# A four-level attention and FFN block: the first batch's loads, copies and early splits rearranged

## The reference

```python
for lvl in range(LEVELS):
    outs.append(_mha(query[:, ::2 ** lvl, :], in_proj_w[lvl], in_proj_b[lvl], out_w[lvl], out_b[lvl]))
current = outs[-1]
for lvl in range(LEVELS - 2, -1, -1):
    current = _upsample_linear(current, outs[lvl].shape[1])
    current = current @ up_w[lvl].T + up_b[lvl] + outs[lvl]
x = _layernorm(x + current)
h = silu(x @ w1.T * s1) * (x @ w2.T * s2)
h = gelu(h @ h1.T * g1); h = gelu(h @ h2.T * g2)
x = _layernorm(x + h @ w3.T * s3)
```

## Time and profile before

| | us |
|---|---|
| median of 3 runs | 4289.43 |
| lowest and highest | 4281.64, 4312.08 |
| the profiled execution, its own time | 4283.97 |
| its span | 4282.2 |
| attention's part of the span, roughly | 0 to 2790 |

### The profile page before, as it was taken

One profiled execution on the slowest core, in us unless ns is written; L12 is line 12 of the kernel. 1 busy time (PEld: TensorE's weight loads), 2 busy tenths in 40 slices (PEclk: granted clock), 3 DMA queues, 4 the chain that ended last, 5 costly groups with the idle time before them and its releaser, 6 DMA issues. The chain is left out here.

```text
span 4282.2 us, 69980 instructions
## 1 busy us (share of the span) xinstructions
PE 3849.3 (90%) x20881; PEld 2139.0 (50%) x20881; DVE 2564.1 (60%) x4681; ACT 2484.3 (58%) x3261; POOL 1212.0 (28%) x1144
## 2 busy tenths in 40 slices
PE   4499989989989999999999999809999999999998
PEld 2234434333433433433333433207887777877887
DVE  2377777787787787787787788553333333333333
ACT  1367767767767767767767767724444434444443
POOL 4234444434534534534434442210000000000000
PEclk8799999999999999999999999959999999999999
DMA  5434343334344344344344343160000000000000
GB/s 176 116 71 103 98 89 88 104 79 103 102 79 104 105 85 93 113 88 85 118 86 91 111 91 57 34 232 12 12 20 11 11 11 21 11 11 11 14 17 11
DMA packets 308844, 307.48 MB, mean 72 GB/s; under 512 B 75168, under 2 KB 285280, under 8 KB 308192
## 3 DMA queue, kind: packets, MB, share of 16 engines
q1 hardware_dynamic: 299200, 293.59, 27.9%
q10 hardware_dynamic: 9216, 8.39, 0.6%
HBM read 202.28 MB, written 96.47 MB: 70 GB/s over the span
## 5 line engine op out<-in xcount | busy, mean ns | idle before, releaser
L760 ACT ACTIVATE a_probs<-a_p_s 128x1024 f32<-128x1024 f32 x1360 | 1324.9, 1020 | 592.0 <-PE a_p_s L1002 584.9
L841 DVE TENSOR_REDUCE a_part_max<-a_p_m 128x1 f32<-128x512 f32 x2048 | 1335.8, 680 | 421.5 <-PE a_p_m L1017 417.2
L1017 PE MATMUL a_p_m<-a_k_st,a_q_st 96*128 96x512 bf16 (+2 forms) x2944 | 1007.3, 375 | 177.8 <-DVE a_part_max L841 73.8
L1397 PE MATMUL p_h<-f_h_hi,f_w_hi 128*128 128x512 f32 x2048 | 811.5, 396 | 40.3 <-issue 38.3
L1002 PE MATMUL a_p_s<-a_q_st,a_k_st 98*128 98x512 bf16 (+2 forms) x2944 | 822.9, 367 | 17.4 <-DMA a_q_st<-a_neg_bf 11.6
L1397 PE MATMUL p_h<-f_h_lo,f_w_hi 128*128 128x512 f32 x2048 | 807.7, 394 | 1.6 <-issue 1.6
L1017 PEld LDWEIGHTS a_p_m<-a_k_st,a_q_st 96*128 96x128 bf16 x2944 | 257.8, 97 | 1072.5 <-DVE a_part_max L841 676.6
L1034 PE MATMUL a_p_o<-a_probs,a_v_aug 128*17 128x512 f32 (+2 forms) x5888 | 727.5, 573 | 0.8 <-ACT a_probs L760 0.8
L1366 DVE TENSOR_TENSOR f_h_lo<-f_h_f,f_h_hi 128x512 fp32r<-128x512 f32 x256 | 177.3, 692 | 723.4 <-ACT f_h_hi L1279 723.4
L841 DVE TENSOR_REDUCE a_row_max<-a_p_m 128x1 f32<-128x512 f32 (+2 forms) x672 | 439.9, 680 | 183.6 <-PE a_p_m L1017 177.7
L1277 ACT ACTIVATE f_h_f<-p_h,f_sc 128x512 f32<-128x512 f32 x256 | 176.6, 690 | 584.4 <-PE p_h L1397 584.3
(11 more groups left out here) (116 smaller groups left out, 4604.5 us busy)
## 6 DMA issues: line engine op xcount, KB each, us to landing
qk_scratch<-a_qk_bf SPq DMA_DIRECT2D x96, 384.0 KB, 2.6
a_w_lo<-wqkv_inner SPq DMA_DIRECT2D x32, 768.0 KB, 4.4
a_q_st<-qk_scratch SPq DMA_DIRECT2D x192, 128.0 KB, 6.2
a_k_st<-qk_scratch SPq DMA_DIRECT2D x192, 128.0 KB, 6.5
a_q_st<-qk_scratch SPq DMA_DIRECT2D x336, 64.0 KB, 2.7
a_k_st<-qk_scratch SPq DMA_DIRECT2D x336, 64.0 KB, 2.7
a_a_lo<-a_attn SPq DMA_DIRECT2D x384, 32.0 KB, 2.0
a_o_lo<-wo_inner SPq DMA_DIRECT2D x24, 512.0 KB, 4.2
```

The source lines that it names most:

```text
L760: act.activation(probs[:, s % 2, 2 * p:2 * p + 2, :], p_s[:, 2 * p:2 * p + 2, :], ACT.Exp, scale=HD ** -0.5).then_inc(exp_done.sem, 1)
L841: dve.reduce_max(out, src, AX.X).then_inc(max_read.sem, 1)
L1017: ins = pe.matmul(p_m[:, n % 2, r * size:(r + 1) * size], q_st[0:ROWS, unit.place, j, q * 128:(q + 1) * 128], k_st[0:ROWS, unit.halves[kb] ...
L1397: ins = pe.matmul(out, a, c, start=first and n == 0, stop=last and n == len(terms) - 1)
```

## The change

The opening of batch 0 is arranged anew.

- x of batch 0 and the weights of level 2 go from the inputs straight into idle room: `x_first` and `w_first` are views of `probs`, free until step 0. The weights of level 1 go early into `w_second`, a view of `attn`; the later load task only waits for it and counts. Rounding and cut read from there in batch 0 (`w_raw`).
- x is loaded, rounded and cut in halves of tokens (0 to 511, 512 to 1023) in place of halves of features, in every batch. In batch 0 the second half is loaded behind the weight copies, and rounded and cut six steps after the first, which puts it between projections 0 and 1 in ScalarE's list. TensorE waits for the second half only at level 0.
- The three constant loads move behind the first weights. `row` has a semaphore of its own. VectorE fills one place of `k_st`'s ones (2x2048), and a DMA repeats it to the seven others; GpSimd's fill goes.
- The four weight copies are issued together before x's second half. wo and the seven copies of x become tasks `xcopy`, at steps 1, 4.2, 7.4 and so on to 23.4.
- Level 3's weights are loaded at -10.9 and projected at -5.7, level 0's at -5.2 and -1.35, with 1.2 steps between its projections. Stack 7 stands at 4.5. In SyncE's list the marker for level 1's weights comes ahead of the store of projection 0.
- Projections 0 to 5 of batch 0 have their second and third pieces made on VectorE. VectorE's shift of `v` is 0.4 in place of 0.3.

```diff
--- before.py
+++ after.py
@@ -210,10 +210,11 @@
+EARLY = 6
...
-    "dve": {"v": .3, "row": .3, "out": .3},
+    "dve": {"proj": .35, "v": .4, "row": .3, "out": .3},
@@ -234,9 +235,9 @@
-    load_at = {2: -36, 1: -22, 3: -11.5, 0: 2.5} if first else {2: CUT_POINT - STEPS + .05}
-    proj_at = {2: -28, 1: -16, 3: 1, 0: 6} if first else {}
-    gap = {2: 1, 1: 1, 3: .5, 0: .5} if first else {2: 1.5, 1: 2, 3: 1.5, 0: 2}
+    load_at = {2: -36, 1: -25.9, 3: -10.9, 0: -5.2} if first else {2: CUT_POINT - STEPS + .05}
+    proj_at = {2: -28, 1: -16, 3: -5.7, 0: -1.35} if first else {}
+    gap = {2: 1, 1: 1, 3: .5, 0: 1.2} if first else {2: 1.5, 1: 2, 3: 1.5, 0: 2}
@@ -262,13 +263,15 @@
-    p.append((load_at[2] - .01, "x", 0))
-    p += [(load_at[2] + 3 + .5 * c, "xcut", c) for c in range(2)]
+    p += [(load_at[2] - .01, "x", 0), (load_at[2] + .02 if first else load_at[2] - .005, "x", 1)]
+    if first:
+        p += [(1 + 3.2 * n, "xcopy", n) for n in range(B)]
+    p += [(load_at[2] + 3 + (6 if first else .5) * n, "xcut", n) for n in range(2)]
...
-        stack_at = {0: at[0] + 2.4, 1: at[1] + 2.4, 2: at[3] + 2.4, 3: at[3] + 2.5, 4: at[5] + 2.4, 5: at[5] + 2.5, 6: at[6] + 2.4, 7: at[10] + 2.25}
+        stack_at = {0: at[0] + 2.4, 1: at[1] + 2.4, 2: at[3] + 2.4, 3: at[3] + 2.5, 4: at[5] + 2.4, 5: at[5] + 2.5, 6: at[6] + 2.4, 7: 4.5}
@@ -317,7 +320,7 @@
-    before = [(STEPS + at, kind, 1, n) for at, kind, n in opening if (kind, n) in early]
+    before = [(STEPS + at, kind, 1, n) for at, kind, n in opening if (kind, n) in early or kind == "xcopy"]
@@ -376,6 +379,8 @@
+        x_first, w_first = probs[:, 0, :, :].rearrange("p (c u) t -> p c (u t)", c=2), probs[:, 1, :, :].rearrange("p h t -> p (h t)")[:, 0:QKVCOLS]
+        w_second = attn[:, :, :].rearrange("p r t -> p (r t)")
@@ -391,11 +396,11 @@
-        w_copied, o_copied = [sig(f"w_copied{n}", 0, 16) for n in range(4)], sig("o_copied", 0, 16)
-        x0_copied, x_copied = sig("x0_copied", 0, 16), sig("x_copied", 0, 16)
+        w_copied, o_copied, x_copied = [sig(f"w_copied{n}", 0, 16) for n in range(4)], sig("o_copied", 0, 16), sig("x_copied", 0, 16)
+        w_early, ones_in = sig("w_early", 0, 16), sig("ones_in", 0, 16)
...
-        const_in, const_done, set_done = sig("const_in", 0, 16), sig("const_done", 0), sig("set_done", 0)
-        x_loaded, x_hi_done, x_lo_done = sig("x_loaded", 1, 16), sig("x_hi_done", 2), sig("x_lo_done", 2)
+        const_in, row_in, const_done, set_done = sig("const_in", 0, 16), sig("row_in", 0, 16), sig("const_done", 0), sig("set_done", 0)
+        x_loaded, x_hi_done, x_lo_done = [sig(f"x_loaded{n}", 1, 16) for n in range(2)], sig("x_hi_done", 2), sig("x_lo_done", 2)
@@ -432,6 +437,10 @@
+        def w_raw(it, n):
+
+            return (w_first, w_second)[n] if it == 0 and n < 2 else w_lo[:, :].bitcast(F32)
+
@@ -459,12 +468,6 @@
-                sp.dma_start(col[:, :, :], cols).then_inc(const_in.sem, 16)
-                sp.dma_start(row[:, :, :], rows).then_inc(const_in.sem, 16)
-                sp.dma_start(ident[:, :], ident_in).then_inc(const_in.sem, 16)
-
-                sp.dma_start(wqkv[W_ORDER[0], :, :], wqkv_in[W_ORDER[0], :, :]).then_inc(w_copied[0].sem, 16)
-                sp.dma_start(xt[0, :, :], xt_in[0, :, :]).then_inc(x0_copied.sem, 16)
@@ -473,36 +476,50 @@
-
...
+                            half = slice(n * W, (n + 1) * W)
...
-                                sp.wait_ge(x0_copied.sem, 16)
+                                sp.dma_start(x_first[:, :, half], xt_in[0, :, half].rearrange("(c p) t -> p c t", p=128)).then_inc(x_loaded[n].sem, 16)
...
-                            hold()
-                            sp.dma_start(x_lo[:, :, :].bitcast(F32), xt[number(it), :, :].rearrange("(c p) t -> p c t", p=128))\
-                              .then_inc(x_loaded.sem, 16)
+                                hold()
+                                sp.dma_start(x_lo[:, :, half].bitcast(F32), xt[number(it), :, half].rearrange("(c p) t -> p c t", p=128))\
+                                  .then_inc(x_loaded[n].sem, 16)
+                        elif kind == "xcopy":
+                            if n == 0:
+                                sp.dma_start(wo[:, :, :], wo_in[:, :, :]).then_inc(o_copied.sem, 16)
+                            else:
+                                sp.dma_start(xt[n, :, :], xt_in[n, :, :]).then_inc(x_copied.sem, 16)
...
-
...
-                            if it == 0:
+                            if it == 0 and n > 1:
...
-                            sp.dma_start(w_lo[:, :].bitcast(F32), wqkv[lvl, :, :]).then_inc(w_loaded.sem, 16)
-                            if it == 0 and n < 2:
-                                for i in (1,) if n == 0 else (2, 3):
+                            if it == 0 and n == 0:
+                                sp.dma_start(w_first, wqkv_in[lvl, :, :]).then_inc(w_loaded.sem, 16)
+                            elif it == 0 and n == 1:
+                                sp.wait_ge(w_early.sem, 16)
+                                sp.sem_inc(w_loaded.sem, 16)
+                            else:
+                                sp.dma_start(w_lo[:, :].bitcast(F32), wqkv[lvl, :, :]).then_inc(w_loaded.sem, 16)
+                            if it == 0 and n == 0:
+                                sp.dma_start(col[:, :, :], cols).then_inc(const_in.sem, 16)
+                                sp.dma_start(ident[:, :], ident_in).then_inc(const_in.sem, 16)
+                                sp.dma_start(row[:, :, :], rows).then_inc(row_in.sem, 16)
+                                sp.dma_start(w_second, wqkv_in[W_ORDER[1], :, :]).then_inc(w_early.sem, 16)
+                                sp.wait_ge(zeroed.sem, 2)
+                                hold()
+                                sp.dma_start(k_st[ROWS:ROWS + 2, 1:HALVES, :, :].rearrange("p b h t -> p b (h t)"),
+                                             k_st[ROWS:ROWS + 2, 0, :, :].rearrange("p h t -> p (h t)").unsqueeze(1).broadcast_to((2, HALVES - 1, HG * W))).then_inc(ones_in.sem, 16)
+                                for i in (1, 2, 3, 0):
...
-                            elif it == 0 and n == 2:
-                                sp.dma_start(wo[:, :, :], wo_in[:, :, :]).then_inc(o_copied.sem, 16)
-                                for b in range(1, B):
-                                    sp.dma_start(xt[b, :, :], xt_in[b, :, :]).then_inc(x_copied.sem, 16)
@@ -614,10 +631,8 @@
-                pool.memset(k_st[ROWS:ROWS + 2, :, :, :], 1.0).then_inc(set_done.sem, 1)
+                pool.memset(minus_half[:, :], -0.5).then_inc(set_done.sem, 1)
...
-                pool.memset(minus_half[:, :], -0.5).then_inc(set_done.sem, 1)
-                pool.wait_ge(set_done.sem, 3)
@@ -625,18 +640,19 @@
-                            pool.tensor_tensor(out=x_lo[:, n, :], in0=x_lo[:, n, :].bitcast(F32), in1=x_hi[:, n, :], op=ALU.subtract)\
+                            half = slice(n * W, (n + 1) * W)
+                            pool.tensor_tensor(out=x_lo[:, :, half], in0=(x_first if it == 0 else x_lo.bitcast(F32))[:, :, half], in1=x_hi[:, :, half], op=ALU.subtract)\
...
-                            pool.tensor_tensor(out=w_lo[:, :], in0=w_lo[:, :].bitcast(F32), in1=w_hi[:, :], op=ALU.subtract)\
+                            pool.tensor_tensor(out=w_lo[:, :], in0=w_raw(it, n), in1=w_hi[:, :], op=ALU.subtract)\
...
-                        elif kind == "proj":
+                        elif kind == "proj" and (it != 0 or n >= EARLY):
@@ -714,21 +730,23 @@
-                act.wait_ge(const_in.sem, 48)
-                act.activation(col_near[:, :, :], col[:, :, CUP:CCOLS], ACT.Copy, scale=0.75).then_inc(up_done.sem, 1)
-                act.activation(col_far[:, :, :], col[:, :, CUP:CCOLS], ACT.Copy, scale=0.25).then_inc(up_done.sem, 1)
-                act.wait_ge(up_done.sem, 2)
...
-                            x_loaded.wait(act, it, 1)
-                            act.activation(x_hi[:, n, :], x_lo[:, n, :].bitcast(F32), ACT.Copy).then_inc(x_hi_done.sem, 1)
+                            half = slice(n * W, (n + 1) * W)
+                            x_loaded[n].wait(act, it, 1)
+                            act.activation(x_hi[:, :, half], (x_first if it == 0 else x_lo.bitcast(F32))[:, :, half], ACT.Copy).then_inc(x_hi_done.sem, 1)
...
-                            act.activation(w_hi[:, :], w_lo[:, :].bitcast(F32), ACT.Copy).then_inc(w_hi_done.sem, 1)
+                            act.activation(w_hi[:, :], w_raw(it, n), ACT.Copy).then_inc(w_hi_done.sem, 1)
+                            if it == 0 and n == 0:
+                                act.wait_ge(const_in.sem, 32)
+                                act.activation(col_near[:, :, :], col[:, :, CUP:CCOLS], ACT.Copy, scale=0.75).then_inc(up_done.sem, 1)
+                                act.activation(col_far[:, :, :], col[:, :, CUP:CCOLS], ACT.Copy, scale=0.25).then_inc(up_done.sem, 1)
```

(28 more changed lines are left out.)

## The result

The changed kernel takes 4190.8 us (median of 4 runs, 4183.3 to 4199.2) against 4291.1 for the kernel before: ratio 0.976, 95% interval 0.9726 to 0.9794. The forecast was 4220, from 4200 to 4250. The direction held; the time lies under the range. The profiled execution took 4192.32 us where the one before took 4283.97, so 91.7 us are to be accounted for, not 64.

The account below looks back on a forecast made before the run. TensorE bounds the kernel, busy 3849.3 of 4282.2 us, so only its idle stretches in the first batch can shrink. Unit 2 ending 66.5 us sooner, less 2.5 for copies, gives 4284 - 64 = 4220 us, range 4200 to 4250.

Parts of the forecast that it names:

- the FFN unchanged: Feed-forward part after attention: expected to stay as before, with no term in the sum.
- 66.5 - 2.5 = 64 us: Whole gain: unit 2 of batch 0 ends 66.5 us sooner, less 2.5 us charged for the copies.
- The 2.5 us charged for the copies: Steps 1 to 23.4 of batch 0: total cost of spreading 9.4 MB of wo and x copies on SyncE's queue.
- The third hole: Batch 0, 113.3 to 139.4 us: TensorE works 1.64 of 26.1 us behind bunched copies; closes, some 16 us given back.
- the fourth: Batch 0, 163.5 to 218.2 us: TensorE works 28.14 of 54.7 us while eight level 0 projections hold its order.
- The 4.0 us: Before batch 0's first maximum: VectorE's two splits and ScalarE's reading between them delay it 4 us, bounds 2 and 6.
- The rule: Opening: two-SBUF-input VectorE instructions and SBUF-reading GpSimd instructions exclude each other; the cut waits 1.5 us, giving 4221.5.
- (a): Rival, batch 0: copies only moved, delaying stores or stacks; 31 us in place of 2.5, 4248.5; chance 0.13.
- (b): Rival, step 0 to unit 2: level 0 projections' stall stays through store lockstep; 16 us back, 4236; chance 0.16.
- (c): Rival, later batches: x's load and cuts in halves cost 11.7 us each, 82 us in seven, 4302; chance 0.03.
- (d): Rival, opening: no store late and projections between steps hide wholly; 12 + 2.5 us more gained, 4205; chance 0.10.
- my unknowns: x half 1 at 20 to 27, projection 6 5 to 13, VectorE 2 to 6, later batches -7 to +14 together.

Follow-up runs that it names:

- the bunch: Changed kernel with the copies of wo and x 1 to 7 issued all at once behind the third weight load: 4211.4 us, ratio 0.9813.
- the old places: Changed kernel with loads and projections of levels 3 and 0, and stack 7, at their places before the change: 4212.0 us, ratio 0.9816.
- the two orders: Copies bunched and levels 3 and 0 at old places, both put back in the changed kernel with TensorE's branch outside the FFN loop: 4186.0 us.
- the branch outside: TensorE's choice between two and three weight planes taken once outside the FFN loop: changed kernel 4138.3 us, again 4139.1; kernel before 4229.5 us.
- 252 more: Changed kernel with 252 never-run instructions in TensorE's untaken branch ahead of the FFN loop: 4202.4 us, ratio 0.981.
- the inner copies: Changed kernel with first x half and first level's weights loaded through inner DRAM copies: 4189.8 us; with TensorE's branch outside the FFN loop, 4145.7 us.

## Why the prediction was wrong, point by point

**The step that failed** is "the FFN unchanged". The sum, "66.5 - 2.5 = 64 us", has no term behind attention. I had read the FFN as a part that the change doesn't touch, and that is right of its work and wrong of its time: 21.4 of the 27.7 us by which 91.7 exceeds 64. The stalls stood in the view of waits of the kernel before, 39.9 us with "issue" as releaser, and I priced nothing on them. With them 4220 becomes 4199, still a little high. That the stalls could go I could not read from that view alone: it took four instructions more in TensorE's program, and the runs show that these, and nothing in the order of the opening, moved them.

**The other 6 us** are in attention. Unit 2 ended at 149.6 where I had 151.7. From there to unit 7 it took 74.4 us; I kept the 78.3 of the earlier trace rows. The runs separate these: 74.3 with the bunch, 77.6 with the old places, so those 3 to 4 us belong to the projections that now lie ahead. The 2.5 us charged for the copies didn't show by unit 7, when all of them are issued (the last at 192.7). Behind unit 7 2.3 us of the 72.5 are lost in the later batches, within their scatter.

**The opening's clock was right, step by step.** First matmul 12.3 (11.2), second half of x rounded at 22.5 (23), projection 2 at 30.0 (30.4), first maximum 54.8 (53.7), step 0 at 105.15 (104 to 105), unit 7 at 224 (near 230). Later batches keep their length: the last units of batches 1 to 6 are 327 to 335 us apart both before and after.

**What the parts are worth** I had right less by reason than by sum. The third hole closes by the copies' spread (20.6 us) and the fourth by the places (21.2). Of the 43.5 us beside the two orders the direct loads of the first x and weights give 6.6 and VectorE's split nothing. The rest, some 37 us by medians and 17 to 20 at unit 7, belongs to what no run put back by itself: level 1's weights loaded early (projection 2 comes 29.8 us sooner, the first matmul only 13.1), the constants behind the weights, GpSimd's fill, x in halves. Which of them gives how much is not shown. The 4.0 us by which I let VectorE's split delay the maxima don't exist: without it the first maximum is 0.4 us sooner.

**The port.** The rule of the Trainium skill, page "SBUF — State Buffer", section "Who interferes with whom", is now borne out by rows. A subtraction of two SBUF tensors on VectorE takes 1.57 us in place of 0.69; it was issued at 24.99 beside GpSimd's cut of x's second half, which ended at 26.02. The cast has one SBUF input, so the rule as I gave it doesn't reach it, and it was held all the same: 0.43 us alone and 3.52 beside GpSimd's 3.42 us cut, ending as that ends. The same section of the Trainium skill names casts among the instructions that can take both ports. I had also written that no such VectorE instruction ran beside GpSimd in the old opening. One did, the sum in `row` (two SBUF inputs), and took 0.42 us beside the memset, which reads nothing; in the changed kernel it takes 3.06 beside the cut of the first weights. But it was VectorE that waited, not the cut of level 1's weights, and nobody waited for VectorE: SyncE's store of that projection stood behind stack 0 until 31.69. So the rule holds, and the forecast without its 1.5 us was the right one.

**The rivals.** (a) fell: the spread copies are hidden. (b) fell, and the old places show what it would have cost, 29 us at unit 7. (c) fell by the batches' unchanged length. (d) was nearest in time, but it expected 14.5 us more from the opening, which gave 6 to 8, and knew nothing of the FFN: it came near for the wrong reason.

**The range.** I wrote that my unknowns add to about 15 us each way. As listed they add to 15 us downward and 25 upward (4 + 5 + 2 + 14). Neither takes in 4190.8.

**What stays open.** With the FFN alike, the opening alone is 4229.5 - 4139.1 = 90 us by medians, but 73 between the two profiled executions and 70 at unit 7. The profiled execution of the kernel before with the branch outside was 12.7 us under its own median and that of the changed one 5.0 over its own, so the gap is scatter that one profile of each cannot follow.

## What to carry to other kernels

An idle time with "issue" as releaser, at the same place of each turn of a loop and with a slow matmul behind it, can be a cost of the code's layout, as it was here: see whether the instruction queue's packets fall into the stalls and grow with them, look for a long branch that isn't taken inside the loop, and take the choice outside. As long as such stalls are there, any edit that changes the length of TensorE's program ahead of the loop can move the time (here by 0.5%), so compare kernels part by part before a gain is credited to the edit. In an opening, order the one DMA queue by who waits for what stands behind: a bunch of large copies costs the first stack behind it nearly their whole transfer (here 28.5 us for 9.4 MB).

## What the runs showed that was not expected

- Four instructions that never run: -21.3 us in the FFN (1472.8 to 1451.5). 252 more: +22.1.
- A stall of 4 to 5 us costs more than itself. Five cost 40.3 us with the clock: 23.4 of standing, the rest mostly slower matmuls behind.
- TensorE goes to its higher level at a different moment from execution to execution, and attention's opening moves with it. With the branch outside, one run of the same kernel had step 0 at 99.9 us and the other at 104.8. Timelines of TensorE at 20 us, the changed kernel and then the first of those two:

```profile
20.32 0.42 PE L938 MATMUL a_p_a<-a_x_hi,a_w_lo 128*128 128x256 f32 x1
```

```profile
20.26 0.28 PE L938 MATMUL a_p_a<-a_x_hi,a_w_lo 128*128 128x256 f32 x1
```

The same matmul at nearly the same time takes 0.42 or 0.28 us, after the same 25 matmuls. The granted clock of the stretch from 12 to 24 us is 1.00 in both, so the matmuls' own durations must be read beside it. Step 0 of a single profile is known to some 5 us only, which is also why the 5.0 and 6.9 us of the inner copies are one number.
